# Flamingo layer pair on one Trainium2 core: maxima of the first query group over six PSUM banks, and its first row block normalised ahead of the other three

## What is computed

```
x = x + tanh(g_ffn[0])   * L0_ffn(layernorm(x))
x = x + tanh(g_xattn[1]) * attention(query=layernorm(x), keys and values=ctx_2048, mask)

Q = split_heads(query, 8) * 32 ** -0.5
logits = Q @ K.T + b + mask
weights = softmax(logits)
out = weights @ V
```

## Time and profile before

| what | value |
|---|---|
| median of 3 runs | 1308.63 us |
| lowest, highest | 1307.96, 1308.99 us |
| the profiled execution's own time | 1309.08 us |
| its span in the profile | 1307.0 us |
| busy share PE / DVE / ACT / POOL | 89 / 40 / 35 / 37% |
| last work of the first experts | 380.9 us |
| first piece of group 0 reduced | 396.67 us |
| last piece of group 0 reduced, `split` begins | 434.02 us |

### The profile page before, as it was taken

One profiled execution on the slowest core, in us unless ns is written; L12 is line 12 of the kernel. 1 busy time (PEld: TensorE's weight loads), 2 busy tenths in 40 slices (PEclk: granted clock), 3 DMA queues, 4 the chain that ended last, 5 costly groups with the idle time before them and its releaser, 6 DMA issues.

```text
span 1307.0 us, 19231 instructions
## 1 busy us (share of the span) xinstructions
PE 1166.2 (89%) x7062; PEld 853.6 (65%) x7062; DVE 525.9 (40%) x1281; ACT 463.8 (35%) x1067; POOL 478.5 (37%) x498
## 2 busy tenths in 40 slices
PE   4866999999968899999999999999948999999986
PEld 3665999999955444544545454434427989888885
DVE  5664222211127786766657676532052001000100
ACT  4111222211101345555555555664312333333331
POOL 1241111111113275755767575571002333333331
PEclk9956999999986699999999999999977999999998
DMA  6254878888840000000000000013005999999994
GB/s 212 69 188 168 289 293 289 298 292 319 313 165 4 1 1 1 1 17 1 1 1 17 1 1 17 9 41 133 1 1 192 315 307 317 309 304 309 301 277 135
DMA packets 48504, 193.10 MB, mean 148 GB/s; under 512 B 7930, under 2 KB 28796, under 8 KB 32412
## 3 DMA queue, kind: packets, MB, share of 16 engines
q1 hardware_dynamic: 35886, 170.93, 36.5%
q0 software_dynamic: 10464, 18.36, 5.8%
q10 hardware_dynamic: 2062, 2.60, 0.6%
HBM read 175.48 MB, written 16.38 MB: 147 GB/s over the span
## 4 chain that ended last, share of the span: by engine, by line
PE 68%; DMA 13%; DVE 9%; issue 4%; ACT 2%; POOL 2%; SPq 1%; ACTq 0%; POOLq 0%; DVEq 0%
PE PQ L412 18%; PE PB L428 11%; DMA out<-Z,SI 10%; PE PB L519 8%; PE PQ L504 7%; PE PB L488 5%; PE PQ L558 4%; PE PB L290 4%; PE PB L509 4%; DVE Z L923 4%; PE PQ L488 3%; DMA Z<-xn,SI 2%; PE PQ L290 1%; DMA V<-in_ctx 1%; PE PB L321 1%
## 5 line engine op out<-in xcount | busy, mean ns | idle before, releaser
L412 PEld LDWEIGHTS PQ<-Z,WS 128*128 128x128 f32 x2720 | 324.0, 194 | 21.2 <-issue 14.7
L412 PE MATMUL PQ<-Z,WS 128*128 128x128 f32 x2720 | 328.9, 278 | 9.8 <-issue 8.8
L428 PE MATMUL PB<-WS,Z 128*128 128x256 f32 x992 | 234.4, 380 | 0.0
L923 DVE TENSOR_REDUCE Z<-PB 128x1 f32<-128x402 f32 x340 | 183.4, 567 | 89.0 <-PE PB L488 87.7
L428 PEld LDWEIGHTS PB<-WS,Z 128*128 128x128 f32 x992 | 179.2, 191 | 19.2
L504 PE MATMUL PQ<-QS,KS 128*128 128x512 f32 x416 | 173.4, 438 | 7.3 <-ACT Z L1135 4.5
L1073 ACT ACTIVATE Z<-PQ,WS 128x128 f32<-128x128 f32 x312 | 88.9, 368 | 196.7 <-PE PQ L412 196.7
L504 PEld LDWEIGHTS PQ<-QS,KS 128*128 128x128 f32 x416 | 77.3, 191 | 105.3 <-issue 60.3
L488 PE MATMUL PB<-KS,QS 128*128 128x402 f32 x340 | 132.6, 401 | 14.2 <-DVE Z L923 5.8
L1135 ACT ACTIVATE WS<-PQ 128x512 f32<-128x512 f32 x208 | 109.4, 605 | 83.9 <-PE PQ L504 83.7
L1135 ACT ACTIVATE Z<-PQ 128x512 f32<-128x512 f32 x208 | 109.6, 604 | 81.9 <-PE PQ L504 81.8
(11 more groups left out here) (240 smaller groups left out, 1202.4 us busy)
## 6 DMA issues: line engine op xcount, KB each, us to landing
WS<-in_w SPq DMA_DIRECT2D x62, 1024.0 KB, 6.2
WS<-in_w SPq DMA_DIRECT2D x23, 2048.0 KB, 8.0
WS<-in_w SPq DMA_DIRECT2D x39, 1028.0 KB, 7.0
xn<-WS SPq DMA_DIRECT2D x32, 128.0 KB, 1.8
X<-in_x SPq DMA_DIRECT2D x4, 512.0 KB, 12.1
WS<-yd SPq DMA_DIRECT2D x4, 512.0 KB, 5.7
out<-X SPq DMA_DIRECT2D x4, 512.0 KB, 3.0
dep_d<-Z SPq DMA_DIRECT2D x13, 128.0 KB, 1.7
```

Of the source, the lines that this page charges most:

```text
L412: t = e.matmul(bank[:, j * P:j * P + P], w[:, k, o:o + P], FXT[i % 2][:, k * P:k * P + P], start=k == 0, stop=k == 1)
L428: t = e.matmul(y, FS[c % 4][:, j * P:j * P + P], w[:, 4 * n + j, :], start=n == 0 and j == 0, stop=n == 1 and j == 3)
L923: e.tensor_reduce(MP[j % 2][:, i:i + 1], PB[bank_of["pc", r]][:, 0:PIECE], AX.X, ALU.max).then_inc(v_pc, 1)
```

## The change

In group 0 the ring has six banks (4, 5, 3, 0, 1, 2) in place of three; banks 0 to 2 belong to `scores` later, and are idle then. Behind group 0 the ring goes back to (4, 5, 3) at its first place. The first three `scores` wait until the ring's last user of their bank has been read.

The first row block gets its normalisation alone: `added(0)`, `inv_std(0, 1)`, `power` on one column, `query_norms(0, 1)`; then come the three others, with a second `inv_std`, `power` on three columns and `query_norms(1, 4)`. POOL does `queries(0)` between the two powers. All later counts of v_pw, p_pw and v_qn are one higher.

```diff
-            ring = {"banks": (4, 5, 3), "n": 0, "free": dict(ring0["free"])}
+            ring = {"banks": (4, 5, 3, 0, 1, 2), "n": 0, "free": dict(ring0["free"])}
...
-                        b = ring["banks"][ring["n"] % 3]
+                        b = ring["banks"][ring["n"] % len(ring["banks"])]
...
                 if g >= 3:
                     e.wait_ge(a_p, g - 2)
+                else:
+                    e.wait_ge(*ring["free"][g])
...
             for _ in maxima(0):
                 pass
+            ring["banks"], ring["n"] = (4, 5, 3), 0
...
-            for c in range(4):
+            added(0)
+            inv_std(0, 1)
+            e.wait_ge(p_pw, 7)
+            query_norms(0, 1)
+            for c in range(1, 4):
                 added(c)
-            inv_std(0, 4)
-            e.wait_ge(p_pw, 7)
-            query_norms(0, 4)
+            inv_std(1, 4)
+            e.wait_ge(p_pw, 8)
+            query_norms(1, 4)
...
-                e.wait_ge(v_qn, 2 if qg else 1)
+                e.wait_ge(v_qn, 3 if qg else min(c, 1) + 1)
...
-            power(rst[:, 0:4], 7)
-            for j in range(6):
+            power(rst[:, 0:1], 7)
+            queries(0)
+            power(rst[:, 1:4], 8)
+            for j in range(1, 6):
                 queries(j)
```

More of the change, by code:

```diff
@@ L936, in rest_of_x @@
                 if piece == 43:
-                    e.wait_ge(p_pw, 8)
+                    e.wait_ge(p_pw, 9)
                     query_norms(4, NC)
@@ L968, in normed @@
                 if c == 0:
-                    e.wait_ge(p_pw, 9)
+                    e.wait_ge(p_pw, 10)
                 if c == 12:
-                    e.wait_ge(p_pw, 10)
+                    e.wait_ge(p_pw, 11)
                 if c >= 4:
@@ L1251, in maxima @@
                         if n == 1 and t4 == 2 and i == 5:
-                            power(rst[:, 4:NC], 8)
+                            power(rst[:, 4:NC], 9)
                         if i == (12 if n == 1 and t4 == 2 else 6) and 4 * n + t4 + 2 < 32:
@@ L1258, in scores @@
                 if n == 7 and kc == 1 and hh == 0:
-                    power(rst[:, 0:12], 9)
+                    power(rst[:, 0:12], 10)
                 if not on_pool(kc) or kc == 0:
@@ L1273, in _ @@
             interleaved(maxima, scores, lambda *a: None, lambda n: None, lambda n: None, lambda n, part: None, lambda c: None)
-            power(rst[:, 12:NC], 10)
+            power(rst[:, 12:NC], 11)
             e.wait_ge(d_res, 64)
```

## The result

| what | before | with the change |
|---|---|---|
| median of 7 runs | 1308.63 us | 1297.24 us |
| lowest, highest | 1306.81, 1310.71 us | 1294.71, 1303.47 us |
| ratio, with its 95% interval | | 0.9923 (0.9895 to 0.9952) |
| span of the profiled execution | 1307.0 us | 1292.9 us |

The medians differ by 11.4 us, the ratio says 10.1 (6.3 to 13.7), and the forecast was 7.6.

A forecast was written before the change was run, and what follows sets the result against it. It took a chain of small steps before the first reduction, then VectorE's reductions with gaps in group 0, as the bound. Start 3.3 plus gaps 4.47 gave 7.8 us off 1308.63; with 0.2 left for the clock, 1301.0, range 1299.5 to 1304.6.

The forecast's parts named there:

- Who bounds group 0: Group 0: VectorE sets the pace at 0.485 us a piece, except in two places a block; gaps total 4.72 us.
- Six banks: Group 0's ring: blocks 1 to 3 lose all gaps, 0.25 us stays in block 0; gain 4.47 us.
- at whatever clock: Group 0, blocks 1 and 2: 7.9 us each, VectorE never waiting for TensorE, whichever clock TensorE is granted.
- The first row block: Start, before the first reduced piece: normalising one block ahead of three brings the first reduction to 393.4, gaining 3.3 us.
- The sum and its way to the end: Start 3.3 plus gaps 4.47 gives 7.8 us, reaching the end except 0.2 us left for the clock's phase.
- The last sign of the prediction: Behind group 0: distance from block 3's split to the first score (2.3 us) and to the end as before.
- Rival (c), the clock: TensorE's clock behind group 0: dips cost or give 1 to 3 us, or make the kernel slower, 1311.3 or more; chance 0.04.
- (a): Start: VectorE's adds wait 2.8 us in all, so it gives only 0.9; 1303.2 us. Chance 0.13, with all in between.
- (b): Group 0: six banks give little because TensorE is the limit at its lower clock; 1305.3 us, chance 0.06.
- (d): Before the end: an unseen wait takes the gain back and the time is the same; chance 0.05.
- How the numbers follow: Whole kernel: chances and range; own case 1299.6 to 1302.5 at 0.68, range 1299.5 to 1304.6, faster at 0.90.

The follow-up runs named there:

- without the stream: Kernel before and changed kernel, each with the weights of the second experts' tiles 2 to 38 not loaded: 1289.41 us and 1281.58 us.
- The kernel with the early table: Changed kernel plus one small exp on ScalarE in group 0, loading the exp table early: 1298.69 us; without the second experts' 74 weight transfers 1282.88 us.
- the first block alone: Changed kernel with group 0's ring back to three banks: 1305.33 us, ratio 0.9968 to the kernel before; without the 74 weight transfers 1287.75 us.
- The delayed kernel: Changed kernel with 24 fills of an unused tile on VectorE ahead of the first add: 1318.46 us.

## Why the prediction was wrong

By its own steps:

- **Who bounds group 0.** Right. VectorE reduces a piece each 0.485 us, and with six banks nothing stops it.
- **Six banks.** Right, 4.69 us against 4.47. Block 1 took 7.85 us (7.88 worked out). In block 0 0.12 us of the gap stayed, where I took 0.25. The clause "at whatever clock" held: blocks 1 to 3 had a mean granted clock of 1.00, 0.78 and 0.72, so partly 2.4 and partly 1.2 GHz, and each took 7.85 or 7.86 us.
- **The first row block.** Right, 3.39 against 3.3. The contention that I priced at 0.2 us for each of two adds and 0.15 on POOL's path was 0.2 on one add and 0.06 on a cast (0.35 in place of 0.29). The Trainium skill (SBUF — State Buffer, "Who interferes with whom") says that a VectorE instruction with two SBUF inputs contends with a GpSimd instruction that reads SBUF, and that the order of issue decides which of them is blocked. The trace agrees: the add of 0.61 us at 388.56 began within POOL's last operation (388.44 to 388.90) and ended 0.27 behind it. So did the add of 1.36 us in the earlier trace rows: it ended 0.28 behind POOL. The add at 387.57 began 0.12 before the end of POOL's long operation (387.69); it too ended 0.27 behind it, which for an add of 0.39 is no loss.
- **The sum and its way to the end.** Right: 7.8 us worked out, 8.08 in the two stretches, 7.83 and 7.64 at the end where the stream was left out. The last sign of the prediction, a distance from the split to the end "as before", did not hold in the first profile: it was 4.23 us shorter.
- **Rival (c), the clock.** The swing is real and worth what I gave it, 1 to 3 us. It goes both ways in one and the same kernel: the kernel before had 455.15 us from last split to router in one profile and 452.50 in the next.
- **The other rivals.** None came: the start gave 3.39 us and not the 0.9 of (a), the six banks 4.69 and not the nothing of (b), and without the stream the gain reached the end whole, against (d).
- **How the numbers follow.** This step failed. I set the forecast against a median of three runs that lay within 1.0 us, and built the range from the costs of the change alone. The kernel's executions scatter by 11 to 15 us (standard deviation 3.2 over 71 runs of before, 3.4 over 13 of the changed kernel). From this I estimate that a median of a few such runs may lie 2 us off on either side, and a difference of two such medians 3. The sentence "The best case is 3.43 + 4.72 = 8.15, 1300.5, less 1 us for a dip that goes: 1299.5." left out the term that was largest. With 3 us for it at both ends the range would have been 1296.5 to 1307.6; that is worked out afterwards, with the scatter known. And I wrote that both later stages "begin when group 0 has ended, and neither waits for anything of fixed time. No transfer is under way." That looks at the attention groups alone. Behind them lie the second experts with their chained output writes, which took 287.7 to 298.7 us from first to last in eight profiles. The page had the row for it: DMA out<-Z,SI with 10% of the chain that ended last.

That the first median fell at 1297.24 is in part luck of the draw. The seven runs lay in two heaps, four from 1294.71 to 1297.24 and three from 1302.99 to 1303.47. The second median of the same kernel was 1300.11, inside the range; the median of all 13 runs is 1298.35, still 1.2 us below it.

Over all runs the changed kernel's mean is 1299.8 us (13 runs) and that of before 1308.9 (71 runs), a difference of 9.1 us with a standard error of 1.0. Of this 8.1 is shown by the stages. The 1.0 left is one standard error; a gain of more than some 3 us beside the two stretches is excluded. I take the rest for chance, but did not show that it is. The kernel with the early table, which gains nothing without the stream, lies 10.5 us below before in its six runs with it, so a small gain that needs the stream stays open. The runs without the stream show none: mean against mean 7.6 us there, with a standard error of 0.5.

## What to carry to other kernels

Where one engine drains banks at a fixed pace and another fills them in bursts, count the burst: the ring must hold as many results as the drainer consumes while the filler does other work (here 0.74 + 0.72 = 1.46 us from the start of the transposes to the first reduction behind them, three reductions of 0.485), and a bank whose reader is a third engine should not be wanted soon. Banks that a later stage owns are free before it, and lending them out costs three waits. Where a whole group waits for the first block's preparation, do that block alone, and follow the engine that now waits twice: its second wait must be over before the first work arrives. And before a forecast is made to a few tenths of a per cent, ask which part of the chain is a transfer that competes with others; its scatter belongs into the range, and leaving that part out of both kernels showed a gain of 8 us, with four and five runs, to a standard error of 0.8 us.

## What the runs showed of the hardware

- Writes that add to memory and are chained one behind the other take a varying time beside a weight stream of some 300 GB/s: from issue to landing 3.6 us at the least, 6.3 at the median and 10.2 at most in the kernel before, against 3.5, 3.8 and 3.9 without the stream. From the first write to the last the 39 tiles took 287.7 to 298.7 us with the stream in eight profiles and 273.1 without in six: 15 to 26 us more, different in each execution.
- POOL's power takes 0.57 us for one column and 0.88 for three, on the line through 1.04 for four and 2.29 for twelve.
- TensorE's granted clock behind group 0 fell into few patterns. Four executions, of the kernel before (with and without the stream), of the changed one without it and of the first block alone, still ran at 2.4 GHz at the last split; they reached the first exp 3.72 us behind it and the router of the second experts 452.5 to 452.7 us behind. In the two microseconds behind the split their granted clock was 0.84 to 0.87. The delayed kernel was at 2.4 GHz at the split too, but at 0.67 behind it, and had 4.32 and 455.15 us. Where TensorE was at 1.2 GHz in those two microseconds it was 4.42 us, and 453.1 to 455.4 (3.13 us, and 455.4 to 455.6, with the early table). One kernel can show either.
